# Turning z times L to tokens by a fixed product, and copying second factors on chip, in a two-layer adaLN and FFN kernel with LoRA

## The reference

```python
# layer 0
c0 = einsum('bsi,boi->bso', x, W0[id0[b]])                  # one of 8 matrices per sample
y  = c0 @ W1.T + b1 + low_rank0(c0)                          # LoRA of rank 16, adapter by segment, none for segment 0
x1 = x + y
# layer 1
c1 = x1 @ W2.T + b2 + scale[id1[b]] * (x1 @ A1[id1[b]].T) @ B1[id1[b]].T
H  = c1 @ W3.T + b3
z  = c1 @ A                                                  # 32 columns
H_slice     = H[:, 1::2, :8]
delta_slice = z[:, 1::2] @ L.T                               # L = LiMEs, 8 experts x 32
logits  = 0.5 * H_slice / max|H_slice| + 0.5 * delta_slice / max|delta_slice|   # max over everything
probs   = softmax(logits)
weights = probs * sigmoid((probs - second largest) / 0.5), normalized, repeated for both tokens of a pair
out = x1 + H + ((z * (weights @ L)) @ Bmat) * 0.5
```

## Time and profile before

| | us |
|---|---|
| runs | 134.25, 135.06, 137.37; median 135.06 |
| the profiled execution | 134.48 |
| its span, first to last instruction | 132.5 |
| TensorE busy | 120.9 (91%) |
| VectorE busy | 83.6 (63%) |
| ScalarE busy | 56.5 (43%) |
| GpSimd busy | 22.5 (17%) |
| moved by DMA | 23.04 MB, mean 174 GB/s |

### The profile page before, as it was taken

How to read it: one execution, slowest core, us unless ns; L and a number is a source line. 1 busy time by engine, 2 the same in 40 slices (tenths; PEclk the granted TensorE clock), 3 DMA queues, 4 the chain that set the end, 5 groups by cost and what they waited for, 6 DMA issues and landing times.

```text
span 132.5 us, 1890 instructions
## 1 busy us (share of the span) xinstructions
PE 120.9 (91%) x703; PEld 103.3 (78%) x703; DVE 83.6 (63%) x172; ACT 56.5 (43%) x94; POOL 22.5 (17%) x30
## 2 busy tenths in 40 slices
PE   6999999999829999999818999999989999999992
PEld 2488777888719999998717898999978878688891
DVE  0599299848967496754299376087995557431671
ACT  3374499459977374905914613153051011031000
POOL 3077815040047505000041000000000000000000
PEclk9999999999995999999997799999999999999999
DMA  3999965999389993896980000000000000000673
GB/s 108 383 393 413 404 251 140 332 398 327 95 357 380 294 329 101 287 376 203 409 326 4 0 0 0 5 0 0 0 0 0 5 0 0 0 0 0 227 272 137
DMA packets 7752, 23.04 MB, mean 174 GB/s; under 512 B 800, under 2 KB 1184, under 8 KB 7488
## 3 DMA queue, kind: packets, MB, share of 16 engines
q1 hardware_dynamic: 4784, 13.06, 26.7%
q0 software_dynamic: 2624, 9.44, 20.3%
q10 hardware_dynamic: 336, 0.44, 0.9%
HBM read 18.64 MB, written 4.29 MB: 173 GB/s over the span
## 4 chain that ended last, share of the span: by engine, by line
PE 59%; DMA 15%; DVE 15%; issue 4%; ACT 3%; SPq 1%; ACTq 0%; DVEq 0%
PE bank L851 45%; DMA b_rows<-c_lo 7%; DVE w_lo L542 5%; DMA x_in<-in_x 5%; DMA b<-b_rows 4%; PE bank L963 3%; PE bank L953 3%; DVE c_row L747 2%; PE bank L956 2%; PE bank L959 2%; DVE m_lo L581 2%; PE bank L888 1%; DVE bm_parts L740 1%; DVE x_lo L533 1%; ACT w_hi L381 1%
## 5 line engine op out<-in xcount | busy, mean ns | idle before, releaser
L336 POOL DMA_INDIRECT w_in<-in_W,rows_i x16 | 16.8, 1048 | 30.4 <-DVE w_lo L542 12.5
L851 PE MATMUL bank<-c_hi,w_hi 128*128 128x256 f32 x64 | 18.8, 294 | 2.9 <-DMA b<-b_rows 2.9
L542 DVE TENSOR_TENSOR w_lo<-w_in,w_hi 128x1024 fp32r<-128x1024 f32 x16 | 19.1, 1220 | 2.8 <-ACT w_hi L381 2.7
L851 PE MATMUL bank<-c_lo,w_hi 128*128 128x256 f32 x64 | 18.8, 294 | 0.0
L851 PE MATMUL bank<-c_hi,w_lo 128*128 128x256 f32 x64 | 18.8, 294 | 0.0
L381 ACT CAST w_hi<-w_in 128x1024 fp32r<-128x1024 f32 x16 | 16.1, 1047 | 3.5 <-DMA w_in<-in_W,rows_i 3.5
L851 PE MATMUL bank<-w_hi,x_hi 128*128 128x512 f32 x32 | 13.7, 428 | 3.1 <-issue 2.9
L851 PEld LDWEIGHTS bank<-c_hi,w_hi 128*128 128x128 f32 x64 | 12.8, 200 | 3.2 <-issue 3.0
L851 PE MATMUL bank<-m_hi,x_hi 128*128 128x512 f32 (+1 forms) x36 | 13.8, 385 | 0.0
L851 PE MATMUL bank<-m_hi,x_lo 128*128 128x512 f32 (+1 forms) x36 | 13.2, 367 | 0.0
L851 PE MATMUL bank<-w_hi,x_lo 128*128 128x512 f32 x32 | 13.2, 413 | 0.0
(11 more groups left out here) (181 smaller groups left out, 241.9 us busy)
## 6 DMA issues: line engine op xcount, KB each, us to landing
w_in<-in_W SPq DMA_DIRECT2D x5, 512.0 KB, 4.9
x_in<-in_x SPq DMA_DIRECT2D x4, 512.0 KB, 7.3
out_dram<-w_in SPq DMA_DIRECT2D x7, 256.0 KB, 3.0
be<-be_rows SPq DMA_DIRECT2D x1, 1120.0 KB, 5.1
b<-b_rows SPq DMA_DIRECT2D x1, 1024.0 KB, 4.7
w_in<-in_W SPq DMA_DIRECT2D x1, 1024.0 KB, 9.1
be_rows<-low_t SPq DMA_DIRECT2D x1, 840.0 KB, 5.2
b_rows<-c_lo SPq DMA_DIRECT2D x1, 768.0 KB, 4.6
```

Source lines behind the costliest of these rows:

```text
L336: nc.gpsimd.indirect_dma_start(w_in[:, slot, half * h:half * (h + 1)], None, W0, row).then_inc(w_landed[b][h], 16)
L542: nc.vector.tensor_tensor(part(w_lo[:, b % 2], h), raw(b, h), f32(part(w_hi[:, b % 2], h)), ALU.subtract).then_inc(w_lo_done, 1)
L851: ins = mm(o, st, mv, start=start and n == 0, stop=stop and n == len(parts) - 1)
```

## The change

1. L A is not formed at the beginning: TensorE's product, ACT's copy and the small load `al` go. `small` has NS = 40 columns. In the turn to tokens, z's 2 x 40 rows are multiplied by a fixed matrix `sel` (80 x 48, built on the host and loaded with `late`): it adds the hi and lo parts and makes z L from z. The transposes become products, and DVE's addition goes.
2. `b0` and `be` are copied within SBUF, 16 DMAs of 32 rows each, with no DRAM in between. The rows have another order (`bits`, `by_rank`, and `turn_rows` without `by_pair`), so that each copy takes 32 neighbouring rows. `b0_landed` is one semaphore for each pair. DVE waits for all copies of b0 before `c0_low(2)`; ACT waits for all copies of be before `low1_high(0)`.
3. W1 is no longer held until g0 has landed, and the load of x pair 2 no longer until W0[3] has.
4. On SP the load of x pair 3 stands before the copies of be. The last columns of be are split earlier (ACT and DVE, behind `low0` of pair 0 instead of behind the split of ae), and the split of Bmat stands before `x1_high(2, 1)` / `x1_low(2, 1)`.

```diff
-NS = R + 2 * NE
+NS = R + NE
+NT = R + 2 * NE
-LATE = {"bias": D, "bm": D, "lr": R}
+LATE = {"bias": D, "bm": D, "lr": R, "sel": NT}
...
 (SP)
-            sp.wait_ge(g0_landed, 16)
             sp.wait_ge(w2_lo_done, 4)
             sp.wait_ge(w3_lo_done, 4)
...
-            def spread(parts, rows, stored):
-                src = f32(parts[:, 0]).unsqueeze(1).to_broadcast([P, G - 1, parts.shape[-1]])
-                sp.dma_start(rows[0:G - 1].rearrange("g p d -> p g d"), src).then_inc(stored, 16)
-                sp.dma_start(rows[G - 1], f32(parts[:, 1])).then_inc(stored, 16)
-            def gathered(rows):
-                return rows.rearrange("g (k i) d -> (g k) (i d)", i=NP)
+            def spread(t, parts, i, landed):
+                for g in range(G):
+                    sp.dma_start(f32(t[K2 * g:K2 * (g + 1), i]),
+                                 f32(parts[K2 * i:K2 * (i + 1), 0 if g < G - 1 else 1])).then_inc(landed, 16)
...
 (ACT, at the beginning)
             act.wait_ge(early_landed, 16)
-            act.wait_ge(al_ready, 1)
-            nc.scalar.copy(small[:, :, R + NE:NS],
-                           bank[4][:, 0:C * NE].rearrange("p (c e) -> p c e", e=NE)).then_inc(small_done, 1)
-            act.wait_ge(small_done, 1)
             nc.scalar.copy(small_parts[:, :, 0:NS], small).then_inc(small_hi_done, 1)
...
 (ACT, low1_high)
                 if i == 0:
-                    act.wait_ge(be_stored, 32)
+                    act.wait_ge(be_landed, 16 * NP * G)
...
 (DVE)
             x_low(2)
+            for i in range(NP):
+                dve.wait_ge(b0_landed[i], 16 * G)
             c0_low(2)
...
-                ps = bank[ZR_BANK[h]][:, 0:4 * 2 * NS].rearrange("p (b n) -> p b n", n=2 * NS)
-                nc.vector.tensor_copy(zr[:, 4 * h:4 * h + 4], ps[:, :, 0:NS]).then_inc(zr_step, 1)
-                dve.wait_ge(zr_step, h + 1)
-                nc.vector.tensor_tensor(zr[:, 4 * h:4 * h + 4], ps[:, :, NS:2 * NS], zr[:, 4 * h:4 * h + 4],
-                                        ALU.add).then_inc(zr_done, 1)
+                ps = bank[ZR_BANK[h]][:, 0:4 * NT].rearrange("p (b n) -> p b n", n=NT)
+                nc.vector.tensor_copy(zr[:, 4 * h:4 * h + 4], ps).then_inc(zr_done, 1)
...
 (PE)
-            for c in range(C - 1):
+            for c in range(C):
                 m_chunk(c)
-            pe.wait_ge(al_landed, 16)
-            for c in range(C):
-                last = mm(bank[4][:, NE * c:NE * (c + 1)], a_t[:, c], l_t, start=True, stop=True)
-            last.then_inc(al_ready, 1)
-            m_chunk(C - 1)
...
             def turn_small(i):
+                pe.wait_ge(late_landed, 16)
                 pe.wait_ge(zt_saved, i + 1)
                 for b in (2 * i, 2 * i + 1):
-                    at = 2 * NS * (b % 4)
-                    last = nc.tensor.transpose(bank[ZR_BANK[b // 4]][:, at:at + 2 * NS], z_t[:, S * b:S * (b + 1)],
-                                               ident[0:2 * NS, 0:2 * NS])
+                    at = NT * (b % 4)
+                    last = mm(bank[ZR_BANK[b // 4]][:, at:at + NT], z_t[:, S * b:S * (b + 1)], sel, start=True, stop=True)
```

More of the change, by code:

```diff
@@ L52, in place, with build @@
         at += w
-def build(nc, x, W0, W1, W23, g0, g1, scale, early, al, late, b0_rows, be_rows, out):
+def build(nc, x, W0, W1, W23, g0, g1, scale, early, late, out):
     ctx = ExitStack()
@@ L165, in build @@
         x_landed = [sem(f"x_landed{i}") for i in range(NP)]
-        early_landed, al_landed = sem("early_landed"), sem("al_landed")
+        early_landed = sem("early_landed")
         g0_landed, g1_landed, s_landed = sem("g0_landed"), sem("g1_landed"), sem("s_landed")
-        b0_stored, be_stored, w3_landed = sem("b0_stored"), sem("be_stored"), sem("w3_landed")
-        b0_landed, be_landed = sem("b0_landed"), sem("be_landed")
+        w3_landed = sem("w3_landed")
+        b0_landed, be_landed = [sem(f"b0_landed{i}") for i in range(NP)], sem("be_landed")
         late_landed = sem("late_landed")
@@ L478, in _ @@
             low0_high(0)
+            act.wait_ge(bes_summed, 1)
+            nc.scalar.copy(be_parts[:, 0, D:], bes_f[:]).then_inc(bes_hi_done, 1)
             w_high(3)
@@ L490, in _ @@
             nc.scalar.copy(ae[:, :, 0:NS], ae_f[:]).then_inc(ae_hi_done, 1)
-            act.wait_ge(bes_summed, 1)
-            nc.scalar.copy(be_parts[:, 0, D:], bes_f[:]).then_inc(bes_hi_done, 1)
             for i in range(2, NP):
@@ L504, in _ @@
                 c0_high(2 * i + 1)
+                if i == NP - 1:
+                    act.wait_ge(late_landed, 16)
+                    nc.scalar.copy(bm_parts[:], bm4).then_inc(bm_hi_done, 1)
                 x1_high(i - 1, 1)
-            act.wait_ge(late_landed, 16)
-            nc.scalar.copy(bm_parts[:], bm4).then_inc(bm_hi_done, 1)
             low0_high(NP - 1)
@@ L701, in _ @@
             low0_low(0)
+            dve.wait_ge(bes_hi_done, 1)
+            nc.vector.tensor_tensor(be_parts[:, 1, D:], bes_f[:], f32(be_parts[:, 0, D:]),
+                                    ALU.subtract).then_inc(bes_done, 1)
             w_low(3)
@@ L730, in _ @@
                 c0_low(2 * i + 1)
+                if i == NP - 1:
+                    dve.wait_ge(bm_hi_done, 1)
+                    for a in (1, 3):
+                        at = slice(R * a, R * (a + 1))
+                        nc.vector.tensor_tensor(bm_parts[at], bm4[at], f32(bm_parts[at]),
+                                                ALU.subtract).then_inc(bm_done, 1)
                 x1_low(i - 1, 1)
@@ L736, in _ @@
             low1_low(NP - 2)
-            dve.wait_ge(bm_hi_done, 1)
-            for a in (1, 3):
-                at = slice(R * a, R * (a + 1))
-                nc.vector.tensor_tensor(bm_parts[at], bm4[at], f32(bm_parts[at]), ALU.subtract).then_inc(bm_done, 1)
             dve.wait_ge(w3_landed, 16)
@@ L939, in layer_low1, with turn_rows @@
                 low_rank(bank[7][:, 0:2 * S], a1, i, x_hi[:, i], x_lo[:, i]).then_inc(low1_ready, 1)
-            def turn_rows(o, rows, by_pair):
+            def turn_rows(o, rows):
                 for c in range(C):
                     to = chunk(o[:], c)
-                    last = nc.tensor.transpose(to.rearrange("p (i k) -> p k i", k=K2) if by_pair else to, chunk(rows, c),
+                    last = nc.tensor.transpose(to, chunk(rows, c),
                                                ident[:])
@@ L1150 @@
     small[:, :, R:R + NE] = turned(W3[0:NE])
+    sel = np.zeros((2, NS, NT), np.float32)
+    sel[:, :, 0:NS] = np.eye(NS, dtype=np.float32)
+    sel[:, 0:R, NS:NT] = v["L1_ffn_LiMEs"].T
     b3 = np.zeros((P, 1), np.float32)
@@ L1174 @@
                         ids=np.ascontiguousarray(ids).view(np.float32)),
-        "al": packed(AL, R, a_t=A.T, l_t=v["L1_ffn_LiMEs"].T),
-        "late": packed(LATE, P, bias=bias, bm=np.concatenate([v["L1_ffn_Bmat"]] * 4), lr=np.concatenate([v["L1_ffn_LiMEs"]] * NB)),
+        "late": packed(LATE, P, bias=bias, bm=np.concatenate([v["L1_ffn_Bmat"]] * 4), lr=np.concatenate([v["L1_ffn_LiMEs"]] * NB),
+                       sel=sel.reshape(2 * NS, NT)),
     }
```

61 lines of the change are left out of this document (25 added, 36 removed).

## The result

| | before | after |
|---|---|---|
| runs beside each other, median | 136.04 (4 runs, 134.25 to 137.37) | 129.28 (4 runs, 128.84 to 131.15) |
| the profiled execution | 134.48 | 128.84 |
| its span | 132.5 | 127.1 |
| TensorE busy | 120.9 | 118.3 |
| moved by DMA | 23.04 MB | 20.79 MB |

The ratio is 0.959 (95% interval 0.951 to 0.967): faster, by 5.4 us of span where 10.0 were forecast. The forecast time was 124.7, the range 122.5 to 128.8, and the median, 129.28, lies above it.

The account below looks back on a forecast made before the run. TensorE, busy 120.9 of 132.5 us, was taken as the bound, with its gaps and slow-clock stretches to win. Terms summed to -10.0: span 122.5, run 124.5, said as 124.7 after a third of 0.6; range 122.5 to 128.8.

Parts of the forecast that it names:

- (a): Start of the kernel: product of L and A and its ScalarE copy go, the 0.16 us gap closes; -1.2 us.
- (b): W1 issued at about 12 us without waiting for g0, so W0[2] lands sooner; -0.6 us, between 0 and -0.8.
- (c): Before layer_b(0,0): b0 copied on chip lands in time; gap of 2.87 goes, -2.9 us, its slow stretch -1.6.
- (f): W0[4] in W1's slot lands at 43.2, TensorE waits for c_row near 44.4; +0.6 us, 0 to +2.9 by landing.
- (e): Before layer_a(6): the second long gap goes, -3.9 us, and its slow stretch, -1.7; margin roughly 1 us.
- (h): bm operations moved before last round's x1_low: stall of about 0.6 at layer_low1(2), 0.62 gap closes; 0 us, -0.6 to +0.6.
- (g): Turn of z: eight transposes become products, 16 instructions at 0.125 us each; +1.3 us, from +0.7 to +4.4.
- (d): New waits for copies of b0 and be, 0.45 us per issue, be landing near 47: free, 4 us to spare.
- W0[4] is late: Rival: W0[4] lands at its long end, TensorE stalls 2.9 us, low clock costs 1.6 more; 128.6 us, chance 0.13.
- third rival: SP's queue: copies are slow, be lands late; from 1.05 us a copy over 2% slower; chance 0.05.
- the case of the dearest copies: Copies at 1.31 us each, the dearest issue: be lands at 71, 10 us later, time 145 us.
- the first three chances: Forecast 0.62, W0[4] late 0.13, second gap back in part 0.15; given together as 0.91 for faster by over 2%.

## Why the prediction missed

Step by step, from starts of the same work in the two profiles (before less after, so that differences of neighbours give each step):

| step | forecast | measured | from |
|---|---|---|---|
| (a) L A gone | -1.2 | -2.0 | layer_a(0): 20.79, now 18.78 |
| (b) W1 sooner | -0.6 | with (c) | |
| (c) first gap | -2.9 | -3.5 with (b) | layer_b(0,0): 40.02, now 34.53 |
| (c) its slow stretch | -1.6 | -1.5 | the turn behind it: 44.71, now 37.74 |
| (f) W0[4] | +0.6 | +4.4 | end of layer_b ahead of the 0.65 gap: 65.7, now 63.1 |
| (e) second gap | -3.9 | -3.3 | layer_a(6): 69.92, now 63.99 |
| (e) its slow stretch | -1.7 | -1.6 | the turn after it: 79.53, now 71.98 |
| (h) bm | 0 | 0 | first turn of z: 98.37, now 90.86 |
| (g) turn of z | +1.3 | +1.0 | two groups, 0.33 each, now 0.83 |
| end of the program | 0 | +1.0 | last operation to end, 2.6, now 3.6 |

The measured steps add up to -5.5, the span gives -5.4. Of (a), 0.4 us is no part of the change that any run shows: the third group of the products of W2 and W3, ahead of all that L A held up, started at 12.54 instead of 12.94, and in the same kernel again at 13.04.

**The step that failed is (f) with (d).** The mechanism of (f) was right to the chain: slot, issue (35.9 and 37.1 forecast, 35.20 and 36.44 measured), the three operations of ScalarE, and c_row as releaser. Its landing was mis-sized, and 3.8 of the 4.6 us by which the span missed the sum are this step. It was taken at the median of the kernel before, 6.1 us, from a stretch without this traffic; the issues of one's own (d) were priced only as time in SP's queue and for their own readers, and called free. They were not free for W0[4]: the runs show 6.6 us without be beside it and 8.5 with. At 6.6 the wait was 1.0 with no slow clock behind it, so the forecast of +0.6 would have been right within half a microsecond. Yet no run got the forecast time by it: with the DMA engines busy from 38 to 60 us, what was taken from W0[4] came back at be or x pair 3. The rival "W0[4] is late" priced this as 128.6 with the slow stretch, and the profiled run took 128.84; of its signs, a gap over 2 us near 43 with the low clock behind it came as written. That the two times agree so closely is partly luck: without the 1.0 us at the end of that execution, which has nothing to do with W0[4], it would be 127.8. The prediction gave this rival 0.13 and named be's copies as the evidence for it, then let "these loads landed in time in most rounds" outweigh them. Those rounds had no copies beside them.

**(d)** was also wrong in size: 0.65 to 0.69 us for a copy instead of 0.45, and the last of be at 55.6 instead of 47. The 4 us to spare were used up and ScalarE waited 2.2 more, but TensorE had enough work in hand and waited only 0.45. The break-even of the third rival, 0.99 us a copy, was not reached. The Trainium skill's "SBUF — State Buffer", The DMA setup-cost knee, was weighed there: its fixed cost of some 2 us, paid one after another, would have made that rival certain. The copies of b0 landed 4.6 us after their issue in the median and those of be 7.2, while a new one was issued every 0.65 to 0.69: a cost in latency, as the prediction read it.

**(c) and (e)** were right in size, slow stretches included (1.5 and 1.6 us behind gaps of 2.87 and 2.92). For (c) the copies were the cause, as forecast; for (e) it was be's earlier place and x pair 3 ahead of it, since be by way of DRAM at that place has no second gap either. **(b)** was forecast at 0.6; the table can't part it from (c), and the run with W1 held leaves it between nothing and 1.8 us. That its worth depends on (c), and is some 4 us without it, was not seen. **(g)** measured 0.104 for an instruction, below the L968 price of 0.125 of a group with 8 moving columns. The Trainium skill's "TensorE: Matmul & The Clock Gate", Terms, with transposes four times faster for fp32, would have given +2.0. Here the same eight blocks take 1.66 us as products and took 0.66 as transposes: 2.5 times, at 80 x 48 instead of 96 x 96. **(h)** came as forecast: 0.65 us of wait ahead of layer_low1(2), and the gap of 0.62 gone. Two sums in the rivals are off by a little: the case of the dearest copies gives 146 rather than 145 with the +1.3 of (g) in it, and the first three chances make 0.90, not 0.91.

What stays open: whether W0[4] loses by bytes, by packets or by its place in the queues. Table and runs show that be beside it costs it 1.7 to 1.9 us as copies and 3.1 as two stores, not why.

## What to carry to other kernels

When a change frees TensorE and pulls work forward, list every DMA that now lies in the same stretch, and price the critical load with them beside it: a landing time read in the kernel before belongs to the traffic of before. Here, wherever the 1.1 MB of be was put between 37 and 55 us, something else was late (W0[4], x pair 3 or be itself), and moving one load within that crowded stretch only moved the wait. Ask also which part of a change removed which wait: for b0 it was the round trip through DRAM that went, for be it was that it was asked for 17 us sooner, behind x pair 3, and with that the way it took did not matter. And parts of a change are not additive: W1 sooner was worth some 4 us at b0's gap with b0 through DRAM, and under 2 us with the copies.
